# Attention rounds of a fused block: another order of instructions on VectorE and ScalarE

## What is computed

```python
h = einsum('bhid,oi,od->bho', x, weighted_sum, weight); h = concatenate([h, txt], axis=1)
# attention: heads of 16, softmax over the 8 batch entries of one position
q, k, v = split(layernorm(h) @ in_proj.T + bias)
attn = softmax(l2norm(q) @ l2norm(k).T * exp(logit_scale)); o = attn @ v * head_scale
h = h + o @ out_w.T + out_b
# feed-forward: a second small attention inside a token, then 8 experts with a softmax gate
h = h + ffn(layernorm(h))
```

## Time and profile before

| | us |
|---|---|
| median of 3 executions | 764.03 (760.64 to 767.45) |
| the profiled execution, its own time | 763.01 |
| its span in the trace | 761.2 |
| VectorE busy | 662.9 (87%) |
| TensorE busy | 701.7 (92%) |
| ScalarE busy | 426.2 (56%) |
| GpSimd busy | 402.9 (53%) |

### The profile page before, as it was taken

The page is one execution under the profiler, slowest core; times in us unless marked ns, Lnnn a source line. Parts: engine busy times, 40 slices in busy tenths (PEclk is TensorE's granted clock), DMA queues, the critical chain, the costliest instruction groups (busy, mean ns, idle before and its releaser), DMA issues.

```text
span 761.2 us, 48123 instructions
## 1 busy us (share of the span) xinstructions
PE 701.7 (92%) x20167; PEld 498.4 (65%) x20167; DVE 662.9 (87%) x1591; ACT 426.2 (56%) x1098; POOL 402.9 (53%) x1094
## 2 busy tenths in 40 slices
PE   4999979988888888877999999999999999999998
PEld 3888856766777677656556666666666666666663
DVE  5789758899999999976779899988998989888986
ACT  4478745777777777853534444444444444444431
POOL 1141245566566667744446655665566656665511
PEclk9999997999999999996999999999999999999999
DMA  9987100000000000000001001100110011001100
GB/s 322 321 288 215 51 1 4 1 0 0 0 0 0 0 0 0 9 19 11 22 19 30 24 17 28 28 24 17 28 28 24 17 28 28 24 17 28 28 16 21
DMA packets 38366, 33.06 MB, mean 43 GB/s; under 512 B 24786, under 2 KB 33570, under 8 KB 38314
## 3 DMA queue, kind: packets, MB, share of 16 engines
q1 hardware_dynamic: 38314, 32.35, 14.1%
HBM read 22.64 MB, written 4.83 MB: 36 GB/s over the span
## 4 chain that ended last, share of the span: by engine, by line
issue 22%; DVE 22%; POOL 21%; PE 19%; POOLq 1%; ACT 1%; DVEq 1%; ACTq 0%
PE bank L193 4%; PE bank L195 4%; PE bank L194 4%; DVE smax L444 3%; POOL qpad L1425 3%; DVE k_t L476 3%; POOL hx L1439 2%; POOL x1b L1444 2%; DVE ss L479 2%; POOL ms L935 2%; POOL cf L925 2%; PE bank L987 2%; PE bank L976 2%; DVE qn L470 2%; DVE pr_t L462 2%
## 5 line engine op out<-in xcount | busy, mean ns | idle before, releaser
L193 PE MATMUL bank<-we_h,h_t_h 128*128 128x512 f16 x296 | 113.6, 384 | 1.1 <-DVE res L1310 0.9
L194 PE MATMUL bank<-we_l,h_t_h 128*128 128x512 f16 x296 | 112.7, 381 | 0.0
L195 PE MATMUL bank<-we_h,h_t_l 128*128 128x512 f16 x296 | 112.7, 381 | 0.0
L1310 DVE SCALAR_TENSOR_TENSOR acc<-bank,gate,acc 128x256 f32<-128x256 f32 x222 | 100.8, 454 | 4.5 <-PE bank L195 4.0
L193 PE MATMUL bank<-tokw_h,x_t_h 128*128 128x256 f16 x256 | 70.8, 277 | 11.7 <-DVE x_t_l L704 11.6
L194 PE MATMUL bank<-tokw_l,x_t_h 128*128 128x256 f16 x256 | 70.7, 276 | 0.0
L195 PE MATMUL bank<-tokw_h,x_t_l 128*128 128x256 f16 x256 | 70.7, 276 | 0.0
L288 PE MATMUL bank<-k_t,q_t 32*32 32x64 f32 x2368 | 41.7, 218 | 25.1 <-DVE k_t L476 25.0
L987 PEld LDWEIGHTS bank<-fpr_t,v 32*32 32x32 f32 x4736 | 46.6, 104 | 21.6 <-issue 21.4
L1194 ACT ACTIVATE junk<-x 128x256 f32<-128x256 f32 x37 | 15.4, 417 | 77.9 <-DVE x L1363 77.9
L288 PEld LDWEIGHTS bank<-k_t,q_t 32*32 32x32 f32 x2368 | 36.5, 107 | 33.5 <-issue 33.5
(11 more groups left out here) (233 smaller groups left out, 2198.8 us busy)
## 6 DMA issues: line engine op xcount, KB each, us to landing
xbuf<-in_x SPq DMA_DIRECT2D x32, 512.0 KB, 5.4
out<-res SPq DMA_DIRECT2D x36, 128.0 KB
we_s<-in_we SPq DMA_DIRECT2D x4, 512.0 KB, 7.3
inw<-in_in_w SPq DMA_DIRECT2D x1, 768.0 KB, 11.6
hn_t_h<-hn_r_h SPq DMA_TRANSPOSE x37, 2.3
hn_t_l<-hn_r_l SPq DMA_TRANSPOSE x37, 2.4
wrep<-in_w_rep SPq DMA_DIRECT2D x1, 512.0 KB, 4.6
h_all<-in_txt SPq DMA_DIRECT2D x1, 512.0 KB
```

The costliest lines, as they stand in the source:

```text
L193: nc.tensor.matmul(dst, a_h(c), b_h(c), start=start and c == 0, stop=False, skip_group_check=onto)
L194: nc.tensor.matmul(dst, a_h(c), b_l(c), start=False, stop=False, skip_group_check=onto)
L195: last = nc.tensor.matmul(dst, a_l(c), b_h(c), start=False, stop=stop and c == chunks - 1, skip_group_check=onto)
L1310: nc.vector.scalar_tensor_tensor(out=(res if e == E - 1 else acc)[:, :], in0=b_we[s % 2][:, k * D:(k + 1) * D], scalar=gate[p][:, e:e + 1] ...
```

## The change

In the steady round, ScalarE takes the squares and the copy of the keys of tile i+2 directly behind the exponentials, in front of mask, moments, values and high halves. VectorE takes the normalised sums ahead of the transposed exponentials, the sums of squares ahead of `qn`, `q_t` and `k_t`, and the addition and the low half of the sums at the end of the round, one round earlier than where the same tile's stood (a new function `lower`). The three small steps behind `ss` stay behind `k_t`. No instruction is added, removed or resized. In the rounds from `JOIN` (36) on, `lower` stays where it was; the other rounds of the join keep divisor and division together.

```diff
--- before.py
+++ after.py
@@ -377,6 +377,12 @@
                     act.wait_ge(a_sub, i + 1)
                     wait(act, a_prt, i)
                     nc.scalar.activation(pr[:, :, :], sc[:, :, :], ACT.Exp).then_inc(a_exp, 1)
+                if real(i, 2):
+                    act.wait_ge(a_qkm, i + 3)
+                    wait(act, a_ss, i + 2)
+                    nc.scalar.activation(sq[:, :, :], b_qk[p][:, :], ACT.Square, scale=1.0 / WS).then_inc(a_sq, 1)
+                    wait(act, p_kpad, i + 1)
+                    nc.scalar.activation(kr[p][:, :], b_qk[p][:, D:2 * D], ACT.Copy, scale=ROOT * ROOT / WS).then_inc(a_qkr, 1)
                 if real(i, 0) and real(i, 1):
                     nc.scalar.activation(b_s[:, :], am_s[:, :], ACT.Copy).then_inc(a_masked, 1)
                 if real(i, -3):
@@ -391,12 +397,6 @@
                     act.wait_ge(a_mean, i - 2)
                     nc.scalar.activation(moment[:, :], hi, ACT.Square, bias=cf_all[:, at, MEAN:MEAN + 1].squeeze(1), scale=1.0 / SH,
                                          accum_out=cf_all[:, at, RS:RS + 1].squeeze(1)).then_inc(a_keep, 1)
-                if real(i, 2):
-                    act.wait_ge(a_qkm, i + 3)
-                    wait(act, a_ss, i + 2)
-                    nc.scalar.activation(sq[:, :, :], b_qk[p][:, :], ACT.Square, scale=1.0 / WS).then_inc(a_sq, 1)
-                    wait(act, p_kpad, i + 1)
-                    nc.scalar.activation(kr[p][:, :], b_qk[p][:, D:2 * D], ACT.Copy, scale=ROOT * ROOT / WS).then_inc(a_qkr, 1)
                 if real(i, 1):
                     act.wait_ge(a_vm, i + 2)
                     wait(act, a_av, i)
@@ -423,6 +423,16 @@
                 nc.vector.scalar_tensor_tensor(out=hj, in0=b_out, scalar=1.0 / WS, in1=hj,
                                                op0=ALU.mult, op1=ALU.add).then_inc(a_h, 1)
 
+            def lower(i):
+
+                if real(i, -1):
+                    dve.wait_ge(a_onh, i)
+                if real(i, -2):
+                    added(i - 2)
+                if real(i, -1):
+                    wait(dve, a_out, i - 1)
+                    nc.vector.tensor_tensor(on_l[:, :, :], b_ot[:, 0:D], on_h[:, :, :], ALU.subtract).then_inc(a_onl, 1)
+
             def divisor(i):
 
                 if real(i, -1):
@@ -447,23 +457,21 @@
                     wait(dve, a_exp, i)
                     nc.vector.tensor_tensor(sc[:, :, :], s3, smax[:, :].unsqueeze(2).to_broadcast([P, H, 32]),
                                             ALU.subtract).then_inc(a_sub, 1)
-                if real(i, -2):
-                    dve.wait_ge(a_onh, i - 1)
-                if real(i, -3):
-                    added(i - 3)
-                if real(i, -2):
-                    wait(dve, a_out, i - 2)
-                    nc.vector.tensor_tensor(on_l[:, :, :], b_ot[:, 0:D], on_h[:, :, :], ALU.subtract).then_inc(a_onl, 1)
+                if isinstance(i, int) and i > JOIN:
+                    lower(i - 1)
                 if early:
                     divisor(i)
+                    divided(i)
                 if real(i, 0):
                     dve.wait_ge(a_exp, i + 1)
 
                     nc.vector.transpose(pr_t[p][:, :, :], pr[:, :, :]).then_inc(a_prt, 1)
                 if not early and part != 2:
                     divisor(i)
-                if part != 2:
                     divided(i)
+                if real(i, 2):
+                    dve.wait_ge(a_sq, i + 3)
+                    nc.vector.tensor_reduce(ss[:, :], sq[:, :, :], AX.X, ALU.add).then_inc(a_ss, 1)
                 if real(i, 1):
                     dve.wait_ge(a_qkr, i + 2)
                     dve.wait_ge(p_rn, i + 2)
@@ -475,10 +483,6 @@
                     dve.wait_ge(p_kpad, i + 2)
                     nc.vector.transpose(k_t[:, :, :], kpad[:, :, :, :]).then_inc(a_qkt, 1)
                 if real(i, 2):
-                    dve.wait_ge(a_sq, i + 3)
-                    nc.vector.tensor_reduce(ss[:, :], sq[:, :, :], AX.X, ALU.add).then_inc(a_ss, 1)
-
-
                     dve.wait_ge(a_ss, i + 3)
                     nc.vector.scalar_tensor_tensor(out=half_ss[:, :], in0=ss[:, :], scalar=1e-24, in1=half_ls[:, :],
                                                    op0=ALU.max, op1=ALU.mult).then_inc(a_half, 1)
@@ -493,6 +497,9 @@
                     dve.wait_ge(a_xth, i + 4)
                     nc.vector.tensor_tensor(xt[1 - p][1][:, :, :], b_xt[:, 0:D], xt[1 - p][0][:, :, :],
                                             ALU.subtract).then_inc(a_xtl, 1)
+
+                if not isinstance(i, int) or i < JOIN:
+                    lower(i)
 
             return body, divisor, divided, added
```

## The result

The changed kernel takes 783.84 us, the kernel before 762.59 (medians of four executions each). The medians lie 21.3 us apart; the ratio of the executions is 1.0269, 95% interval 1.024 to 1.0297, which makes 20.5 us of the kernel before. The forecast was 779, range 768 to 788, slower with a chance of 0.83. The profiled execution of the changed kernel took 781.44 us, the lowest of its four, against 763.01 before; the traces therefore account for 18.4 us.

What follows compares the result with a forecast made beforehand. VectorE was taken to bound the attention before, a loop through three engines' work after: +12.3 in thirty rounds, +2.6 in the first, 0 in the join, +14.9 on 763.0 gives 777.9, forecast 779 us, range 768 to 788.

Steps and rivals of the forecast that it cites:

- the unwidened range: Whole kernel: 774 to 783 us, before widening by the 3 us spread of the runs.
- the handover: Upper end of the range: 0.03 us a round more for handing over between engines.
- The ring: Loop from one `k_t` through scores, query and key product, squares and `ss` to the next: 6.51 us a round, +0.41.
- VectorE's order: VectorE's own steps, 6.05 us, plus 0.18 of wait for the exponentials before `pr_t`: 6.23 a round.
- Same-engine neighbours: VectorE pairs: `ss` no longer directly before `half_ss`, -0.12 us; `rsum` now directly before `on`, +0.12.
- The cover of the exponentials: VectorE: addition and low half no longer stand over the exponentials, so `pr_t` waits 0.18 us a round.
- First rounds and join: Four rounds before the steady ones: +2.6 us, bounds 0 and +4.5; rounds from 35 on: 0, between -0.5 and +0.5.
- the late `ss` of the very first round: Start of the attention: included when the early rounds' sum of +2.3 us was taken as +2.6.
- Order of VectorE binds: Rival: the product is handed over earlier, so VectorE's sequence sets the round, 6.23 at least; about 769 us; chance 0.11.
- The clock did not fall in the loop: Rival judged: longer TensorE pauses lower its clock in every third of thirty rounds; +18, some 797 us; chance 0.06.
- the 1 us named as a sign: Steady rounds: TensorE's pause before the scores over 1 us would show the forecast holds.

Runs made afterwards that it cites:

- The two moves alone: Kernel before, with only the squares moved behind the exponentials on ScalarE and the sums of squares in front of the queries on VectorE: 782.58 us, ratio 1.0237.
- shorter product: Changed kernel without the four low-half matmuls of the query and key product: 769.29 us, ratio 1.0063 to the kernel before.
- sums first: Changed kernel with TensorE taking the weighted sums of tile i-1 ahead of the scores of tile i: 770.19 us, ratio 1.0081.
- sums of squares back: Changed kernel with only `ss` put behind the keys again: 770.93 us, ratio 1.0116.

## Why the prediction was right, step by step

The forecast's sum for the profiled execution was +14.9, the trace has +18.4: 1.0 us more in the loop, 1.1 more in the first rounds and 1.4 more in the join. The median lies 2.4 us above the profiled execution, where the forecast had put 1.0. Together that is the distance from 779 to 783.84. The sum for the upper end of the unwidened range, 12.3 + 4.5 + 0.5 and 0.9 for the handover, leads from 764.03 to 782 and not to 783; nothing else hangs on it.

**The ring.** Forecast 6.51 us a round and +0.41, measured 6.54 and +0.44: right in mechanism and size. The two moves alone give 6.54, and each of three ways of opening the ring (shorter product, sums first, sums of squares back) brings the round under 6.35. The missing 0.03 is in the main one term, the hand-over from the product to the squares: in every second round it is 0.11 us (product's end 233.43 + .38 = 233.81, squares at 233.92) where the prediction had 0.03 throughout. Timeline of the next round of the changed kernel:

```profile
233.43 0.38 PE L195 MATMUL bank<-inw_h,xt_l 128*128 128x512 f16 x1
...
233.92 0.60 ACT L383 ACTIVATE sq<-bank 128x512 f32<-128x512 f32 x1 [0.31 <-PE bank L195]
```

Over the loop: +13.3 instead of +12.3.

**VectorE's order.** Forecast 6.23 with 0.18 of wait before `pr_t`, measured 6.21 and 6.22 once the ring is open. In the trace of the changed kernel the wait has no row of its own: `on` lies over it. It shows as `on` to `pr_t` .49 (226.67 to 227.16) where the pure interval is .31, and `pr_t` starts 0.03 after the exponentials' end (226.50 + .63).

**Same-engine neighbours.** +0.12 for `rsum` and `on`: 0.11 measured. -0.12 for `ss` and `half_ss`: 6.34 against 6.21 with the pair put back, 0.13. The sentence of the Trainium skill named in the prediction (page "VectorE: DVE Perf Modes", section "The DRAIN you can't avoid"), that the semaphore costs nothing extra, was measured there on a chain of eight copies. It does not hold for these pairs, by the 0.11 and 0.13 us measured here.

**What the prediction did not price.** The cover of the exponentials was seen (0.18 us) only for the whole change. Alone, moving addition and low half costs 0.57 a round. The parts do not add: +0.57 for the low half, +0.11 for the normalised sums and +0.44 for the ring would be 1.12, while the whole change costs 0.44. Each delay in one chain lies under the longer one, and the normalised sums, by standing in front of `pr_t`, fill part of the cover that the other move took away.

**First rounds and join.** Forecast +2.6 and 0, measured +3.7 and +1.4 in the profiled pair. The step "the late `ss` of the very first round" was too small: the first `k_t` came 2.9 us later, since `ss` in front of it waits 3.2 us for the squares of the first product. Timeline of VectorE, changed kernel:

```profile
105.35 0.69 DVE L474 TENSOR_REDUCE ss<-sq 128x32 f32<-128x512 f32 x1 [3.17 <-ACT sq L383]
```

The next round gave 2.1 of it back (`k_t` at 113.41 against 112.63), and the four rounds from there to 144.27 took 30.86 us against 27.95: +2.9 where the sum had +2.3. Windows and TensorE's waits over these four rounds:

```profile
113.41:144.27 30.86, 23.54 (x850) 17.48 (x850) 23.45 (x59) 16.23 (x40) 15.12 (x48) 0.94 0.01 3
```

```profile
PE bank L278 <- issue: 3.7, 2, 2.2
```

The sum came close, but partly by luck, since two of its parts were off in opposite directions. The mean granted clock was 0.94 here and not 0.82, so that the stretches at half speed lost 0.06 x 30.86 = 1.9 us of TensorE's time and not 5.0. And TensorE's stops that no engine released add up to 3.7 us, where the sum had carried over 1.4. The mechanism is shown for the first `k_t` alone: with the old order of the first rounds that gain was gone at tile 3. And with the two moves that close the ring, alone, the `k_t` of tile 5 came at 148.56, 8.0 us later than before, so the ring by itself does not fix this price. The term is right in sign and lies under its bound of 4.5.

The join's +1.4 is not explained: over the kernels run here, the time after the `k_t` of tile 35 lies between 434 and 439 us whatever the change was. It goes together with the mean granted clock of the first 80 us behind that `k_t`: 436.0 to 439.2 us where it was 0.87, 435.7 and 436.3 at 0.89, 434.4 and 434.9 at 0.91. That the clock is the cause is not shown.

**The rivals.** "Order of VectorE binds" would have been 769: short product and sums first, where it is the bound, take 769.3 and 770.2. The clock did not fall in the loop: it stayed at 1.00 over 196 us. TensorE's pause before the scores grew from 0.74 to 0.92 us on average, less than the 1.14 forecast and under the 1 us named as a sign. A part of the added time lies ahead of the transposes of the normalised sums instead, which follow the output product by 0.12 us in the round shown (228.82 to 228.94) and overlapped it before.

## What to carry to other kernels

Where one engine is busy to 97%, ask of every reordering which loop the semaphores close across engines, and add up that loop from start to start; a consumer that was late by a harmless 1.4 us becomes the bound when something the producer needs is put behind it. Read what stands between a hand-over and its return (here, between `sc` and `pr_t`): it is the cover, and instructions taken out of it cost nearly their whole length at their new place (here 0.57 of 0.66 us). The parts of a reordering must be priced together, since the longest loop hides the others.

## What was not expected

An instruction that another engine releases is a little longer than the same one that follows its neighbour: `ss` .69 against .64 us, the squares .60 against .57. For `pr_t` the same was seen, .71 against .67, but with the normalised sums directly in front of it `pr_t` took .70 also where it did not wait for the exponentials (233.07 above, where they ended at 232.53); there the cause is another.

A few microseconds at either end of the stage vary between kernels of nearly the same order: from the `k_t` of tile 0 to that of tile 5, 37.5 us at a granted clock of 0.91 and 40.1 us at 0.87 for kernels that differ in one instruction's place. The clock alone does not set this time: the kernel before took 36.7 us at 0.81, and the two moves that close the ring, alone, 40.8 us at 0.83.
